# Local attention in 96 interleaved steps: scores issued behind the query projection, query transfers in four pieces, scalar chains reordered

## The reference

```python
def attn_layer(x, Wqkv, qs, ksc, Wo):            # 16 heads of 64, windows of 32
    q, k, v = split(x @ Wqkv)
    q = l2norm(q) * qs
    k = l2norm(k) * ksc
    q = q * cos * scale + rotate_half(q) * sin * scale
    k = k * cos * inv + rotate_half(k) * sin * inv
    # window w of the queries sees the keys of windows w-1 and w
    attn = softmax(where(mask, -max, (q @ k.T) * 8.0), -1)
    return (attn @ v) @ Wo
def ffn_layer(x, g, bln, W1, b1, W2, b2):
    a, gate = split(layernorm(x) * g + bln @ W1 + b1)
    return a * gelu(gate) @ W2 + b2
for i in range(6):
    x = attn_layer(shift_tokens(x), ...) + x
    x = ffn_layer(shift_tokens(x), ...) + x
```

## Time and profile before

| | us |
|---|---|
| median of 3 runs (2920.19 to 2924.49) | 2923.6 |
| the profiled execution's own time | 2920.24 |
| its span in the trace | 2918.4 |
| first square of the keys, quarter 0 | 488.3 |
| the same, quarter 95 | 2785.6 |

### The profile page before, as it was taken

One profiled execution on the slowest core, in us unless ns is written; L12 is line 12 of the kernel. 1 busy time (PEld: TensorE's weight loads), 2 busy tenths in 40 slices (PEclk: granted clock), 3 DMA queues, 4 the chain that ended last, 5 costly groups with the idle time before them and its releaser, 6 DMA issues. The chain is left out here.

```text
span 2918.4 us, 47990 instructions
## 1 busy us (share of the span) xinstructions
PE 2071.0 (71%) x18048; PEld 1222.0 (42%) x18048; DVE 1650.5 (57%) x2639; ACT 1384.7 (47%) x2862; POOL 1246.1 (43%) x1015
## 2 busy tenths in 40 slices
PE   4877885466777777777767777677777677776775
PEld 2333333244444444444444444444444344444442
DVE  3577643455565665566556655565566456654643
ACT  0433452344455555545554555455545454554442
POOL 4022001455454554555445545454555455554530
PEclk8888997677888888888888888888888788887887
DMA  5000002322222322223222132212321222122210
GB/s 116 2 1 1 1 2 63 64 49 47 49 49 50 60 48 53 50 48 59 48 55 48 44 62 48 55 44 48 62 48 44 55 48 48 44 48 55 48 30 15
DMA packets 149132, 131.82 MB, mean 45 GB/s; under 512 B 91304, under 2 KB 94952, under 8 KB 148584
## 3 DMA queue, kind: packets, MB, share of 16 engines
q1 hardware_dynamic: 148912, 128.86, 19.7%
HBM read 20.94 MB, written 1.05 MB: 8 GB/s over the span
## 5 line engine op out<-in xcount | busy, mean ns | idle before, releaser
L863 PE MATMUL bank_z<-kpad,qpair 128*32 128x128 f32 x6144 | 348.5, 420 | 609.2 <-issue 576.3
L863 PEld LDWEIGHTS bank_z<-kpad,qpair 128*32 128x32 f32 x6144 | 308.3, 172 | 614.8 <-issue 614.8
L973 ACT ACTIVATE prob<-s_in,lower,rq 128x64 f32<-128x64 f32 x1536 | 528.2, 428 | 44.1 <-DVE lower L1154 43.9
L831 PE MATMUL bank_a<-x_shift,wqk_sb 128*128 128x512 f32 x768 | 444.7, 707 | 47.4 <-DVE pk L1107 34.5
L1066 POOL TENSOR_TENSOR sumq<-sq 128x512 f32<-128x512 f32 x96 | 122.8, 1280 | 809.2 <-ACT sq L1015 809.2
L1133 DVE TENSOR_TENSOR s_in<-bank_z,mask_sb 128x512 f32<-128x512 f32 x96 | 66.2, 689 | 544.0 <-PE bank_z L863 544.0
L850 PE MATMUL bank_y<-zT,wvo 128*128 128x512 f32 x768 | 355.6, 606 | 1.9 <-ACT hid L987 1.9
L1013 ACT ACTIVATE sq<-bank_a 128x512 f32<-128x512 f32 x96 | 57.3, 597 | 629.6 <-PE bank_a L831 629.6
L831 PEld LDWEIGHTS bank_a<-x_shift,wqk_sb 128*128 128x128 f32 x768 | 167.9, 237 | 249.2 <-issue 204.8
L1060 POOL TENSOR_TENSOR sumk<-sq 128x512 f32<-128x512 f32 x96 | 121.8, 1268 | 305.7 <-ACT sq L1007 305.4
L850 PEld LDWEIGHTS bank_y<-zT,wvo 128*128 128x128 f32 x768 | 138.2, 190 | 152.3 <-issue 138.1
(11 more groups left out here) (161 smaller groups left out, 4227.8 us busy)
## 6 DMA issues: line engine op xcount, KB each, us to landing
kpad<-kfin SPq DMA_DIRECT2D x768, 64.0 KB, 2.0
qpair<-qfin SPq DMA_DIRECT2D x768, 64.0 KB, 2.0
wqk_sb<-in_wqkv SPq DMA_DIRECT2D x24, 256.0 KB, 5.6
xk_prev<-xk_own SPq DMA_DIRECT2D x24, 192.0 KB, 2.4
ffn_sb<-in_ffn SPq DMA_DIRECT2D x6, 537.5 KB, 4.3
wv_in<-in_wqkv SPq DMA_DIRECT2D x12, 256.0 KB, 5.0
wo_in<-in_wo SPq DMA_DIRECT2D x6, 512.0 KB, 6.3
xk_prev<-xk_own SPq DMA_DIRECT2D x24, 48.0 KB, 2.1
```

Of the source, the lines that this page charges most:

```text
L831: last = pe.matmul(bank_a[:, half, :], wqk_sb[:, layer_of(u) % 2, part, half, g * P:(g + 1) * P], cols(u), start=True, stop=True)
L863: last = pe.matmul(bank_z[WIN * w:WIN * w + WIN, t // 2, c:c + P], qpair[:, p, at:at + WIN], kpad[:, p, :, at:at + 2 * WIN], start=True, s ...
L973: last = act.activation(prob[:, n % 2, i, :], s_in[:, n % 2, i, :], ACT.Exp, bias=lower[:, n % 2, i:i + 1], scale=rq8[:, n % 2, i:i + 1])
```

## The change

Nothing is added to or taken from the computation; work is written in another order in `step` of each engine.

- SyncE: the queries go first, by four transfers of 64 partitions in place of eight of 32, then the keys by eight. The halves stand in another order in `kpad` and `qpair`, alike in both. The wait for the previous scores (`s_mm`) stands ahead of the queries' transfers.
- TensorE: the output product follows the key projection, the query projection follows it, then weighing, key sums, scores of c, and query sums, now of quarter n and not c. The scores wait for the copy of bank_z of the same step's weighing (`z01_ok`). The feed-forward products that go to bank_f wait for `lnq_ok` only before their third part.
- ScalarE: exponentials come in groups of 5, 3 and 8 around the keys' squares, and both Ln and Exp pairs behind the copy of `zT`.
- GpSimd: `qfin` ahead of `kfin`.
- VectorE: the queries' products, the floor and the sums of exponentials ahead of the mask; the feed-forward's last addition at the end of the step.

```diff
@@ -788,21 +788,19 @@
             def step(s):
                 n = s
                 if quarter(n):
+                    after(sp, qfin_ok, n)
+                    after(sp, s_mm, n - 1)
+                    for p in range(2):
+                        for half in range(2):
+                            sp.dma_start(qpair[64 * half:64 * half + 64, p, :],
+                                         qfin[64 * p:64 * p + 64, half, :]).then_inc(qpair_in, 16)
                     after(sp, kfin_ok, n)
-                    after(sp, s_mm, n - 1)
                     for hh in range(GH):
                         p, e = hh // 2, hh % 2
                         for half in range(2):
-                            to = 64 * e + 32 * half
+                            to = 64 * half + 32 * e
                             sp.dma_start(kpad[to:to + 32, p, e, WIN:WIN + L],
                                          kfin[32 * hh:32 * hh + 32, half, :]).then_inc(kpad_in, 16)
-                    after(sp, qfin_ok, n)
-                    for hh in range(GH):
-                        p, e = hh // 2, hh % 2
-                        for half in range(2):
-                            to = 64 * e + 32 * half
-                            sp.dma_start(qpair[to:to + 32, p, :],
-                                         qfin[32 * hh:32 * hh + 32, half, :]).then_inc(qpair_in, 16)
...
                     project(n, 1, k_mm)
-                if quarter(c):
-                    after(pe, sumq_ok, c)
-                    after(pe, floor_ok, c)
...
-                    after(pe, kpad_in, c, 128)
-                    after(pe, qpair_in, c, 128)
-                    after(pe, z01_ok, c - 3)
-                    scores(c)
-                if quarter(n):
-                    after(pe, sqk_ok, n)
-                    after(pe, pk_ok, n)
-                    project(n, 0, q_mm)
-                    after(pe, sumk_ok, n)
-                    after(pe, lnq_ok, n - 1)
-                    pe.matmul(bank_f[:], same_head[:], sumk[:], start=True, stop=True).then_inc(sumk_mm, 1)
...
-                if quarter(e):
-                    after(pe, pT_ok, e)
-                    after(pe, mask_ok, min(c, QUARTERS - 1))
...
-                    weigh_rows(e)
                 if quarter(h):
...
                     project_out(h)
+                if quarter(n):
+                    after(pe, sqk_ok, n)
+                    after(pe, pk_ok, n)
+                    project(n, 0, q_mm)
...
+                if rows_at(s - 1) is not None:
+                    after(pe, xk_ok, rows_at(s - 1))
+                if quarter(e):
+                    after(pe, pT_ok, e)
+                    after(pe, mask_ok, min(c - 1, QUARTERS - 1))
+                    after(pe, xk_ok, e // GROUPS)
+                    after(pe, prev_in, e // GROUPS, 32)
+                    weigh_rows(e)
+                if quarter(n):
+                    after(pe, sumk_ok, n)
+                    after(pe, lnq_ok, n - 1)
+                    pe.matmul(bank_f[:], same_head[:], sumk[:], start=True, stop=True).then_inc(sumk_mm, 1)
+                if quarter(c):
+                    after(pe, kpad_in, c, 128)
+                    after(pe, qpair_in, c, 64)
+                    after(pe, z01_ok, min(c - 2, QUARTERS - 1))
+                    scores(c)
+                if quarter(n):
+                    after(pe, sumq_ok, n)
+                    after(pe, floor_ok, n)
...
+                    last.then_inc(sumq_mm, 1)
                 if quarter(e):
...
                     after(pe, xnT_ok, u_gate)
-                    after(pe, floor_ok, min(n, QUARTERS - 1))
-                    for j in range(FCH):
-                        last = first_half((bank_z[:, 2, :], bank_z[:, 3, :], bank_f)[j], u_gate, 1, j)
-                    last.then_inc(gate_mm, 1)
+                    first_half(bank_z[:, 2, :], u_gate, 1, 0)
+                    first_half(bank_z[:, 3, :], u_gate, 1, 1)
+                    after(pe, lnq_ok, min(n, QUARTERS - 1))
+                    first_half(bank_f, u_gate, 1, 2).then_inc(gate_mm, 1)
...
-                if quarter(c):
-                    after(act, sumq_mm, c)
-                    after(act, rq8_ok, c - 2)
...
-                    act.activation(rq[:, c % 2], rq[:, c % 2], ACT.Exp, scale=-0.5).then_inc(rq_ok, 1)
+                if quarter(d):
+                    exponentials(d, 5, 8)
...
                 if quarter(d):
-                    exponentials(d, 5, TPB * GH).then_inc(exp_ok, 1)
+                    exponentials(d, 8, TPB * GH).then_inc(exp_ok, 1)
...
-                    after(act, floor_ok, n)
...
                     copy(z[:, 2:4, :], bank_z[:, 2:4, :]).then_inc(z23_ok, 1)
+                if quarter(n):
+                    after(act, floor_ok, n)
+                    act.activation(rk[:], rk[:], ACT.Ln).then_inc(lnk_ok, 1)
+                    after(act, lnk_ok, n)
+                    act.activation(rk[:], rk[:], ACT.Exp, scale=-0.5).then_inc(rk_ok, 1)
+                    after(act, sumq_mm, n)
+                    after(act, rq8_ok, n - 2)
+                    act.activation(rq[:, n % 2], bank_f[:, 0:TPB * GH], ACT.Ln, bias=tiny[:]).then_inc(lnq_ok, 1)
...
                     pool.tensor_tensor(sumq[:], sq[:, 0, :], sq[:, 1, :], ALU.add).then_inc(sumq_ok, 1)
+                    after(pool, pq_ok, n)
+                    after(pool, qpair_in, n - 1, 64)
+                    pool.tensor_tensor(qfin[:, 0, :], pq[:, 0, :], pq[:, 1, :], ALU.subtract)
+                    pool.tensor_tensor(qfin[:, 1, :], pq[:, 2, :], pq[:, 3, :], ALU.add).then_inc(qfin_ok, 1)
                     after(pool, rk_ok, n)
...
-                    after(pool, pq_ok, n)
-                    after(pool, qpair_in, n - 1, 128)
-                    pool.tensor_tensor(qfin[:, 0, :], pq[:, 0, :], pq[:, 1, :], ALU.subtract)
-                    pool.tensor_tensor(qfin[:, 1, :], pq[:, 2, :], pq[:, 3, :], ALU.add).then_inc(qfin_ok, 1)
...
+                if u_add is not None:
+                    after(dve, y_mm, 4 * u_add + 3)
+                    lo, hi = cols(u_add, 0, 64), cols(u_add, 64, P, 1)
+                    dve.tensor_tensor(lo, bank_y[0:64, :], lo, ALU.add)
+                    dve.tensor_tensor(hi, bank_y[64:P, :], hi, ALU.add).then_inc(xa_ok, 1)
+                if quarter(n):
+                    after(dve, q_mm, n)
+                    after(dve, qfin_ok, n - 1)
+                    second_products(n, 0, pq).then_inc(pq2_ok, 1)
+                    after(dve, sqq0_ok, n)
+                    first_products(n, 0, pq).then_inc(pq_ok, 1)
+                    after(dve, sumk_mm, n)
+                    after(dve, kfin_ok, n - 1)
+                    dve.tensor_scalar(rk[:], bank_f[:], 1e-24, None, ALU.max).then_inc(floor_ok, 1)
+                if quarter(d):
+                    after(dve, exp_ok, d)
+                    dve.tensor_reduce(den[:], prob[:, d % 2], AX.X, ALU.add).then_inc(den_ok, 1)
...
                 if quarter(c):
                     after(dve, s_mm, c)
...
-                if quarter(n):
-                    after(dve, q_mm, n)
-                    after(dve, qfin_ok, n - 1)
-                    second_products(n, 0, pq).then_inc(pq2_ok, 1)
-                    after(dve, sumk_mm, n)
-                    after(dve, kfin_ok, n - 1)
-                    dve.tensor_scalar(rk[:], bank_f[:], 1e-24, None, ALU.max).then_inc(floor_ok, 1)
-                    after(dve, sqq0_ok, n)
-                    first_products(n, 0, pq).then_inc(pq_ok, 1)
...
-                if quarter(d):
-                    after(dve, exp_ok, d)
-                    dve.tensor_reduce(den[:], prob[:, d % 2], AX.X, ALU.add).then_inc(den_ok, 1)
-                    after(dve, den_ok, d)
-                    after(dve, pn_ok, d - 1)
-                    dve.reciprocal(rden[:], den[:]).then_inc(rden_ok, 1)
-                if u_out is not None:
-                    after(dve, ff_mm, u_out)
...
-                if u_add is not None:
-                    after(dve, y_mm, 4 * u_add + 3)
...
+                if u_out is not None:
+                    after(dve, ff_mm, u_out)
```

54 lines of the change are left out of this document (20 added, 34 removed).

## The result

The changed kernel takes **2299.3 us** (median of 4 runs, 2296.7 to 2299.8) against 2921.9 us (2919.6 to 2924.5) for the kernel before: a ratio of 0.787, 95% interval 0.785 to 0.788. The forecast was 2221, the range 2165 to 2390. So the time is inside the range and 78 us above the forecast, and 9 us above the own range of the likeliest case. The profiled execution spans 2298.0 us, against 2216 in the sum.

A forecast was written before the change was run, and what follows sets the result against it. The prediction took the loop through SyncE's transfers as the bound. Cutting it saves 675 us over the steps and 27 in the tail from 2918.4, a span of 2216; with run offsets 2221 us, range 2165 to 2390.

The forecast's parts named there:

- the likeliest case: Whole kernel: the forecast of 2221 us, with its own range from 2165 to 2290 and a chance of 0.62.
- The loop through SyncE: Query projection, key finishing, transfers, scores and back: sets the old step at 23.8 us; the new order cuts it.
- The third rival: SyncE's transfers: the keys' landing is still last; at 5 us more, 2364 us; chance 0.02.
- The clock of the scores: TensorE's scores, now in dense work, take 1.9 us in place of 3.57; mean granted clock over 0.93.
- The first rival: TensorE's scores stay at the low clock, 3.57 us each: 2378 us; chance 0.14.
- the fourth: TensorE becomes the bound at the low clock, slower than before: at 60% of steps 3076 us; chance 0.02.
- The walk from the scores to `lower`: VectorE, end of scores to `lower`: 4.0 us, from mask 1.3 and maxima to `lower` 2.7.
- TensorE is now the bound: After the change TensorE's passes, 60.1 us per four steps, plus 6.0 of waits set the cycle; nothing catches up load delays.
- The second rival: Softmax chain from `lower` round to `lower`, 15.0 us, sets the step; one us of stretch gives 2316; chance 0.12.
- The waits of the query projection: TensorE waits for the softmax chain before this projection: gate 0.85, gelu 2.0, output 0.15, rows 0.4 us.
- The four transfers: SyncE's queries by four transfers, not eight: worth nothing in ordinary steps, 2.5 us at each of five layer loads.
- The remark on loads: Feed-forward weight loads on SyncE: one costing much less than 11 us would mean TensorE is not the bound.

The follow-up runs named there:

- Experiment 1: Kernel before with only SyncE's and GpSimd's part of the change, other engines in the old order: 2628.5 us, ratio 0.900.
- Experiment 3: Changed kernel with one wait more, GpSimd's division of the exponentials by their sums held until VectorE has written `lower`: 2202.3 us, ratio 0.754.
- Experiment 5: Changed kernel with the last head of each output product computed twice on TensorE, between key and query projection: 2306.1 us, ratio 0.790.
- experiment 4: Changed kernel with SyncE issuing the next layer's feed-forward weights at the head of the rows step, ahead of queries and keys: 2246.0 us, ratio 0.770.

## Why the prediction was right or wrong

**The loop through SyncE: right.** The idle time ahead of the scores was to fall from 609 under 60 us; it is 23.1. The room of the keys was put at 3.5 at least; it is 6.4. Experiment 1 shows the loop itself: shortening it, with the other engines' order kept, gains 290 us. The third rival falls, since the scores wait for `zT` and not for a transfer.

**The clock of the scores: right.** 1.9 was taken between 1.79 and 3.57; 1.89 is measured, and the mean clock is 0.94 where over 0.93 was named. The first rival (2378) and the fourth (slower than before) fall.

**The walk from the scores to `lower`: mis-sized.** The step read 4.0 us off the timeline of before, 1.3 of mask and 2.7 to `lower`, `lower` itself at 1.12. It is 5.0: 1.76 for `lower` in place of 1.12, and 0.70 for the scaling of `rq` in place of 0.34. A length read beside one neighbour was carried to a place with another: before, `lower` lay beside a product of 1.26, now beside the division of 1.91. Whose end it waits for changed with GpSimd's order, which the change rewrote. Experiment 3 shows that the division's place lies on the path: 97 us. That is not the price of the mis-sizing alone: `lower` fell by 1.58 us, and 0.94 of that the walk had counted. No run puts `lower` back to 1.12.

**"TensorE is now the bound": wrong in the sense in which the prediction used it.** Experiment 5 adds 82 us of work to TensorE ahead of the query projection and costs 7. The second rival, a chain from `lower` round to `lower`, sets three steps in four, and gelu with its table load the fourth; the rival had a chance of 0.12 and a time of 2316 for one us more, which is 17 above the measurement. Its sign, query projections that wait 3 us in each step, was not met: they wait 1.1 to 1.9. The rival was right in the place and in the half of its path: in two steps of four the chain runs through VectorE's own queue and not through exponentials and squares. The prediction had called the two level at 15.0 each and had seen `lower`'s 1.12 as waiting beside GpSimd, but it priced that as a rival and not in the walk. So the measured time lies in the stated range by the rivals' prices; the likeliest case, with its own range to 2290, missed it by 9.

**The waits of the query projection**: 0.85, 2.0, 0.15 and 0.4 by the walk, 1.62, 1.87, 1.10 and 1.38 measured: 3.4 against 6.0 in a cycle. The gelu step is nearly right, as gelu and not `lower` sets it; the other three miss by 0.8 to 1.0, the size of the error in the walk to `lower`. The scores' waits for `zT` are 0.95 in place of 1.75, and the weighing of the rows step waits 0.35 for `xn` in place of 0.85. What is left of the cycle, 61.8, stands against passes of 60.1: 1.7 more than the walk had. The rows of the gelu step above show most of it: the query projection takes 1.89 from start to start (1398.82 to 1400.71) where 1.72 was counted, weighing and key sums 3.12 (1400.71 to 1404.23, less the wait of 0.40) where 2.95 was, the output product 3.60 where 3.53 was, some 0.4 in a step. Added up, 2.6 - 0.8 - 0.5 + 1.7 is the 3.0 of the cycle.

**The sum, term by term.** The cycle of 69.1 in place of 66.1 makes 3.0 x 23.75 = 71 us. The five loads cost 11.1 each on average in place of 11.5 (their two steps less two ordinary ones; the load shown has 26.85 + 19.49, 10.6), -2; experiment 4 has 10.7. The first steps are 1.5 above the cycle's rate where 6 below were estimated, 7.5. Together 76.5, and 1698.0 against 1622 are measured. The rest of the gap of 82 is a start 3.5 later (491.8 against 488.3) and a tail of 61.2 in place of 59. From `xn` to the end 47.0 stayed. Why the start is later was not looked into.

**The four transfers: right in the ordinary step, small elsewhere.** Nothing is gained there; at the loads 2.8 each in place of 2.5, and 21 in all in place of 12, since some 5 us lie in the first steps and the tail.

**The remark on loads** ("one that costs much less than 11 would mean that TensorE is not the bound") was a bad test: the load costs 10.7 though TensorE's own passes are not the bound, since `xnT` stands on ScalarE, ahead of the exponentials of the chain that is.

## What to carry to other kernels

When a wait of a fifth of the time is cut, the next bound can be a chain of small instructions, as it was here; walk it with each duration as it will be beside its new neighbours, not as it was. A VectorE instruction of 16 columns that took 1.76 us and ended with a GpSimd instruction was waiting here, though no view listed it as idle: order the GpSimd instruction behind it if nobody waits for that one. To learn whether an engine is the bound, add work to it, and in more than one place of its step: the answer holds for the place where the work was added. The busy share did not tell it here.

## What the runs showed of the hardware

- A product of 128 x 16 on VectorE with both inputs in SBUF took 0.175 us alone, 1.12 beside a GpSimd product of 128 x 512 and 1.76 beside one of 128 x 1024, with its end within 0.04 us of GpSimd's in 95 rows of 96. The scaling of `rq`, 128 x 16 with one input, took 0.34 in the mean before and 0.63 after. GpSimd's own instructions kept their lengths, 1.27 and 1.90.
- Sixty-four small score passes took 1.89 us in dense work, at a granted clock of 1.00, and 3.57 behind idle time, at 0.50. With the transfers' part of the change alone they stayed at 3.45; the other engines' order brought the rest.
- Issuing a transfer between SBUF places cost SyncE 0.61 us for 128 KB (four in 2.42) and 0.62 for 64 KB (eight in 4.94).
